# Routing of a mixture-of-experts stage: bf16 marks scanned before the matmul, slot tile by rounding, one comparison per row, and work of the next stages moved

## The chip, the cores and the metric

One core of one Trainium2 chip. The metric is device time in microseconds (us) of one execution of the whole program, as the median of several; lower is better.

## The reference

Two layers over x of 4 batches x 512 tokens x 256, each with cross attention and then a feed-forward part. The part that matters here is the feed-forward part of the first layer: eight experts, each token goes to the one with the largest router output.

```python
x = x + jnp.tanh(g_xattn[0]) * _L0_xattn_ref(_layernorm(x), ctx_768, ...)
x = x + jnp.tanh(g_ffn[0])   * _L0_ffn_ref(_layernorm(x), ...)       # the experts
x = x + jnp.tanh(g_xattn[1]) * _L1_xattn_ref(_layernorm(x), ctx_768, ctx_768, ...)
x = x + jnp.tanh(g_ffn[1])   * _L1_ffn_ref(_layernorm(x), ...)

def _L0_ffn_ref(hidden_states, router_w, router_b, w1, w2):
    logits = x @ router_w + router_b
    route = jax.nn.softmax(logits, axis=1)
    max_prob = jnp.max(route, axis=1, keepdims=True)
    max_ind = jnp.argmax(route, axis=1)
    for e in range(num_experts):                     # 8 experts, 256 -> 2 x 1024 -> 256
        a, g = jnp.split(x @ w1[e], 2, axis=1)
        y = jax.nn.silu(a) * g @ w2[e]
        out = jnp.where((max_ind == e)[:, None], y, out)
    return out * max_prob
```

## The kernel before

The 2048 tokens are 16 tiles of 128 (`NT` = 16; a batch is `TB` = 4 tiles). Each engine has its own written program in one block (`@block.tensor`, `@block.vector`, `@block.scalar`, `@block.gpsimd`, `@block.sync`); an engine runs its instructions in the order in which they are written, and waits on semaphores where the code says `wait_ge`. There is no scheduler: where a line stands in an engine's program is where it runs.

The stages are: attention of layer 0 (`attention(0, b, ...)` for b = 0 to 3), in which each batch ends with normalised rows `xn2` (they are also stored to `token_rows` in HBM) and router products of the batch before; routing; the experts; gathering of their outputs; attention of layer 1; the last feed-forward part.

Routing sorts the tokens by expert. `logits` [128, tile, expert] give `onehot`, the mark of each token's expert. A matmul with `before` (1 above the diagonal) counts the marks of earlier tokens in the same tile, one with `ones` the marks of each tile; DVE copies the latter to `count` and scans it over the tiles to `upto`. From `upto` follow the number of 128-row slot tiles of each expert (`tiles_of`, `tile_end`, `slot_base`), and from all of it the position `pos_f` of each token in the sorted list. The list has at most 24 slot tiles (25 are read, `READ_TILES`). To invert it, the kernel makes `in_slot` (bf16, 1 where a token has a given slot within its tile) and `ids` (tile number and row number of the token in the column of its slot tile) and lets PE multiply them: 16 matmuls into `x_bank[0]`, which give `token_f` and `token_of`, the token of each slot. POOL makes the half of `ids` with the row numbers (L573), in the same interval as DVE makes the other.

POOL then gathers the rows of the first two slot tiles by indirect DMA (`gather_rows`), PE turns them (`rows_in`, L960), ACT rounds them to `xs_hi` (L1279), DVE makes the rest `xs_lo` (L1756), and PE starts the first expert product (L976). Every fp32 product with expert weights is made as three products of a high and a low part; ACT makes the high parts of the weights (`upper_first` L1254, `upper_second` L1260), DVE the low parts (`lower_first` L1746, `lower_second` L1751). For the first expert all of that lies between the routing and the first expert tile; ACT's high parts stand behind its copy of the router rows and the exponent `l_exp` (L1248), DVE's low parts behind `token_of` (L1740).

Other work of PE in the stretch: the values of layer 1 (`values_of`, L681 and L682, four batches; DVE spreads them by `spread_values`, L1464), the keys of layer 1 (`keys(1, t_bank)`, L674 and L676; ACT copies them, then makes `k_bd`), and `keep_running(n, o)`: n matmuls of 512 columns whose result nobody reads. Last, SP loads the weights of experts 0 and 1 in this stretch and, when `r_exps` is 2, starts the loop over the later experts.

## Time and profile before

| | us |
|---|---|
| median of 3 runs | 603.48 |
| lowest, highest | 597.16, 603.55 |
| the profiled execution | 595.08 |
| its span, first to last instruction | 592.7 |
| mean granted PE clock (share of full speed) | 0.927 |
| PE busy | 499.5 (84%) |
| DVE busy | 419.2 (71%) |
| ACT busy | 294.2 (50%) |
| POOL busy | 247.1 (42%) |

PE is TensorE, DVE is VectorE, ACT is ScalarE, POOL is GpSimd and SP is SyncE. The profile is of one execution. A timeline row gives the start from the beginning of the span, the time from the first start to the last end of a merged group, the engine, the line of the kernel, the operation and its tiles, and in brackets how long the engine was idle before it and which instruction released it. `x8` means eight instructions in one row. Tiles that share memory are named by one name: `bank`, `s_tile` and `xn` appear for several views, `h_t` for `in_slot` and `ids`, `ew` for the expert weights and for `xn2`.

### The profile page before, as it was taken

Reading aid. Unit: us, or ns where it says so; the run is one execution under the profiler, and the core shown is the slowest. Engines: PE = TensorE matmul, PEld = TensorE weight load, DVE = VectorE, ACT = ScalarE, POOL = GpSimd, SP = SyncE. Lnnn points to the kernel's source line nnn. Section 1 sums busy time; section 2 is a strip of 40 time slices with the busy share of each in tenths; the row PEclk is TensorE's granted clock in tenths of the full one; section 3 lists DMA queues with packets and bytes.
Section 4 is the critical chain, followed back from the end, with each engine's and each line's share of the span. In section 5 each row is a group of like instructions: output and inputs, shape, how many; then the busy total and the mean of one; then the engine's idle time right before and its main releaser. Section 6 shows DMA issues by size and latency. Waiting matters only on the chain.

```text
span 592.7 us, 10230 instructions
## 1 busy us (share of the span) xinstructions
PE 499.5 (84%) x3061; PEld 364.4 (61%) x3069; DVE 419.2 (71%) x809; ACT 294.2 (50%) x521; POOL 247.1 (42%) x314
## 2 busy tenths in 40 slices
PE   7888899896998699899999999944897777649994
PEld 3456658566784278788888888812553544425562
DVE  6598898787546987494756823227979899588992
ACT  1446555362654466483755623203454444427884
POOL 5454263344300311020212110066367878538996
PEclk9989899699698899899999999979599989588999
DMA  7940100100167156555554310022000000000112
GB/s 212 296 147 1 37 0 2 36 0 1 35 215 236 31 161 221 180 178 168 174 178 154 94 35 18 18 81 71 0 1 1 1 1 1 0 0 2 36 35 71
DMA packets 35162, 46.40 MB, mean 78 GB/s; under 512 B 2764, under 2 KB 25304, under 8 KB 35128
## 3 DMA queue, kind: packets, MB, share of 16 engines
q1 hardware_dynamic: 30856, 39.02, 20.4%
q0 software_dynamic: 1680, 4.59, 2.7%
q10 hardware_dynamic: 2592, 2.36, 1.2%
q8 instruction: 18, 0.29, 0.2%
q14 instruction: 16, 0.13, 0.1%
HBM read 38.36 MB, written 7.60 MB: 78 GB/s over the span
## 4 chain that ended last, share of the span: by engine, by line
PE 45%; DVE 28%; POOL 10%; issue 7%; ACT 3%; DMA 2%; SPq 2%; DVEq 1%; POOLq 0%; ACTq 0%
PE s_tile L976 16%; PE bank L997 8%; DVE s_max L1476 4%; DVE p_sum L1490 4%; PE bank L827 3%; DVE probs L1481 3%; PE bank L986 3%; DVE stats L1414 2%; DVE xn L1436 2%; DVE ew L1436 2%; PE bank L711 2%; PE s_tile L1070 2%; POOL probs_t L614 2%; DMA w<-in_L_xattn_W 2%; DVE ew_lo L1746 2%
## 5 line engine op out<-in xcount | busy, mean ns | idle before, releaser
L506 POOL TENSOR_TENSOR probs<-probs,p_rcp 128x1024 f32<-128x1024 f32 x32 | 60.9, 1907 | 94.3 <-DVE p_rcp L1493 94.3
L740 PE MATMUL bank<-ident,probs 128*128 128x128 f32 x256 | 40.4, 309 | 27.0 <-POOL probs L506 25.3
L976 PE MATMUL s_tile<-ew_hi,xs_hi 128*128 128x512 f32 x144 | 59.9, 416 | 3.7 <-DVE ew_lo L1746 2.5
L1167 ACT COPY probs_t<-bank 128x512 f32<-128x512 f32 x64 | 35.0, 588 | 47.1 <-PE bank L740 46.7
L976 PE MATMUL s_tile<-ew_hi,xs_lo 128*128 128x512 f32 x144 | 57.5, 399 | 0.0
L976 PE MATMUL s_tile<-ew_lo,xs_hi 128*128 128x512 f32 x144 | 57.4, 398 | 0.0
L740 PEld LDWEIGHTS bank<-ident,probs 128*128 128x128 f32 x256 | 32.9, 159 | 39.5 <-POOL probs L506 30.1
L564 POOL TENSOR_TENSOR token_now<-token_of,carried 128x1 uint32<-128x1 uint32 x17 | 3.8, 226 | 124.1 <-PE bank L960 124.1
L1764 DVE TENSOR_TENSOR probs_t<-s_tile,probs_t 128x512 f32<-128x512 f32 x36 | 24.8, 689 | 43.1 <-PE s_tile L976 41.7
L1137 ACT ACTIVATE probs<-probs 128x1024 f32<-128x1024 f32 x32 | 33.9, 1058 | 33.8 <-DVE probs L1481 33.7
L1476 DVE TENSOR_REDUCE s_max<-s_tile 128x16 f32<-128x1024 f32 x32 | 38.4, 1199 | 16.6 <-PE s_tile L724 16.5
L1746 DVE TENSOR_TENSOR ew_lo<-ew,ew_hi 128x512 fp32r<-128x512 f32 x64 | 40.4, 686 | 10.3 <-ACT ew_hi L1254 9.4
L1490 DVE TENSOR_REDUCE p_sum<-probs 128x16 f32<-128x1024 f32 x32 | 38.7, 1209 | 6.4 <-ACT probs L1137 6.3
L724 PE MATMUL s_tile<-k_bd,q_t 64*128 64x256 f32 x256 | 40.6, 433 | 3.0 <-ACT q_t L1132 3.0
L997 PE MATMUL bank<-ew_hi,act_hi 128*128 x144 | 42.2, 293 | 0.0
L1481 DVE TENSOR_TENSOR probs<-s_tile,s_max 128x1024 f32<-128x1024 f32 x32 | 39.2, 1225 | 2.0 <-DVE s_max L1476 0.3
L997 PE MATMUL bank<-ew_lo,act_hi 128*128 x144 | 40.5, 282 | 0.0
L997 PE MATMUL bank<-ew_hi,act_lo 128*128 x144 | 40.3, 280 | 0.0
L1254 ACT CAST ew_hi<-ew 128x512 fp32r<-128x512 f32 x64 | 35.5, 619 | 7.5 <-issue 7.5
L1768 DVE TENSOR_TENSOR act_lo<-bank,act_hi 128x512 fp32r<-128x512 f32 x36 | 24.8, 689 | 18.6 <-ACT act_hi L1295 18.6
L1295 ACT CAST act_hi<-bank 128x512 fp32r<-128x512 f32 x36 | 21.2, 588 | 30.4 <-PE bank L986 30.4
L1285 ACT ACTIVATE probs_t<-s_tile 128x512 f32<-128x512 f32 x36 | 21.5, 599 | 28.3 <-PE s_tile L976 24.6
(228 smaller groups left out, 1318.8 us busy)
## 6 DMA issues: line engine op xcount, KB each, us to landing
ew<-in_L_ffn_w SPq DMA_DIRECT2D x32, 512.0 KB, 5.0
...
```

Of the source, the lines that this page charges most:

```text
L506: nc.gpsimd.tensor_tensor(p, p, p_rcp[:, i, :].unsqueeze(2).to_broadcast([P, H, M]), ALU.mult).then_inc(s["p_norm"], 1)
L724: last = nc.tensor.matmul(s_bank[i % 2][g][:, GH * M * m:GH * M * m + GH * M], q_t[rows, m, P * i:P * i + P], flat(k_bd[rows, m, bass.ds(n ...
L740: last = nc.tensor.transpose(t_bank[c][:, P * j:P * j + P], probs[:, i % 2, at:at + P], ident[:])
L976: last = nc.tensor.matmul(o[:], x, w, start=(k == 0 and n == 0), stop=(k == DK - 1 and n == 2))
L997: last = nc.tensor.matmul(y_bank[:, D * par:D * par + D], u, w, start=(c == 0 and n == 0), stop=(c == EK - 1 and n == 2))
L1137: nc.scalar.activation(probs[:, i % 2, :], probs[:, i % 2, :], ACT.Exp).then_inc(att[l]["a_exp"], 1)
L1167: last = nc.scalar.copy(flat(probs_t[:, i % 2, 4 * c:4 * c + 4, :]), t_bank[c][:])
L1254: last = nc.scalar.copy(hi, w)
L1476: nc.vector.tensor_reduce(s_max[:, i, :], s_tile[i % 2][:].rearrange("p (h s) -> p h s", h=H), AX, ALU.max).then_inc(s["v_max"], 1)
L1481: nc.vector.tensor_tensor(probs[:, i % 2, :].rearrange("p (h s) -> p h s", h=H), s_tile[i % 2][:].rearrange("p (h s) -> p h s", h=H), s_ma ...
L1490: nc.vector.tensor_reduce(p_sum[:, i, :], probs[:, i % 2, :].rearrange("p (h s) -> p h s", h=H), AX, ALU.add).then_inc(s["v_sum"], 1)
L1746: last = nc.vector.tensor_tensor(lo, w, hi.bitcast(F32), ALU.subtract)
```

## The change

Routing:

- the marks (`onehot`), `before`, a new `ones_b` and `upto` are bf16. DVE scans the marks themselves over the tiles, row by row, into `upto`, and PE sums that over the 128 rows: two matmuls with `ones_b`, the first added into the same bank as the one with `before`, so that the bank holds the position within the expert at once; the second gives each expert's total. The copy to `count` and two steps on `r_tmp` are gone;
- the slot tile of a position is found by scaling, shifting and rounding (adding and subtracting `ROUND`), in two steps over 16 elements, in place of a comparison with 26 edges and a sum. `in_tile` is then one comparison;
- `in_slot` is made by 16 operations of 128 elements with a per-row scalar, from a bf16 list of slot numbers, in place of four over 512 elements;
- the table of experts by slot tile (`past`, `expert_f`, `last_of`, `expert_of`), `pos` and `weight` come behind the token matmuls or behind `token_of`.

Moved:

- ACT's high parts of the first expert's first weights come ahead of the last router rows; keys come ahead of its second weights;
- DVE's low parts of the first expert, parts 0 to 2, come ahead of the last logits; part 3 stays behind the routing;
- PE makes the values of batches 0 and 1, then the keys, ahead of the last router rows (in other banks), the values of batches 2 and 3 behind the token matmuls; fillers are 6 and 5, 10, 6 where they were 10, 8, 14. A wait for the residual (`v_y`) at the end of the last batch is gone and a full one stands before the keys.

```diff
@@ PE
-                pe.wait_ge(s["v_y"], TB * b + 2)
+                if not (l == 0 and last_batch):
+                    pe.wait_ge(s["v_y"], TB * b + 2)
...
-            for b in range(B):
-                values_of(1, b, s_bank[1][b // 2])
+            for b in range(2):
+                values_of(1, b, s_bank[1][0])
+            pe.wait_ge(att[0]["v_y"], NT)
+            keys(1, (x_bank[0], s_bank[1][1]))
             pe.wait_ge(a_bit, 6)
-            keep_running(10, s_bank[0][0])
-            pe.wait_ge(att[0]["v_y"], NT)
+            keep_running(6, s_bank[0][0])
             router_turn(B - 1)
             router_products(B - 1)
+            keep_running(5, s_bank[0][0])
             pe.wait_ge(r_hot, 1)
-            nc.tensor.matmul(s_bank[0][0][:, 0:NT * E], before[:], flat(onehot[:]), start=True, stop=True)
-            nc.tensor.matmul(s_bank[0][1][:, 0:NT * E], ones[:], flat(onehot[:]), start=True,
-                             stop=True).then_inc(r_mm, 1)
-            keys(1, t_bank)
-            keep_running(8, x_bank[1])
+            nc.tensor.matmul(s_bank[0][0][:, 0:NT * E], before[:], flat(onehot[:]), start=True, stop=False)
+            pe.wait_ge(r_hot, 2)
+            nc.tensor.matmul(s_bank[0][0][:, E:NT * E], ones_b[:], upto[:, :, 0:NT - 1].rearrange("p e t -> p t e"),
+                             start=False, stop=True)
+            nc.tensor.matmul(s_bank[0][1][:, 0:E], ones_b[:], upto[:, :, NT - 1:NT].rearrange("p e o -> p (e o)"),
+                             start=True, stop=True).then_inc(r_mm, 1)
+            pe.wait_ge(r_lg, B)
+            keep_running(10, x_bank[1])
+            pe.wait_ge(a_k, 2 * DK)
...
             last.then_inc(r_mm, 1)
-            pe.wait_ge(a_k, 2 * DK)
-            keep_running(14, x_bank[1])
+            for b in range(2, B):
+                values_of(1, b, s_bank[1][1])
+            keep_running(6, x_bank[1])
             pe.wait_ge(v_vbd, 8)
@@ ACT
-            router_rows(B - 1)
-            act.wait_ge(r_v, 2)
-            nc.scalar.activation(l_exp[:], r_tmp[:], ACT.Exp).then_inc(r_exp, 1)
...
+            act.wait_ge(att[0]["t_y"], NT)
             for p in range(4):
                 upper_first(0, 0, p)
+            router_rows(B - 1)
+            act.wait_ge(r_v, 3)
+            nc.scalar.activation(l_exp[:], r_tmp[:], ACT.Exp).then_inc(r_exp, 1)
+            act.wait_ge(p_kbd, DK * B)
+            keys(1, (x_bank[0], s_bank[1][1]))
             for q in range(2):
                 upper_second(0, 0, q)
@@ DVE
+            spread_values(1, 0, s_bank[1][0])
+            for p in range(3):
+                lower_first(0, 0, p)
             router_logits(B - 1)
...
+            for e in range(E):
+                last = nc.vector.tensor_tensor_scan(upto[:, e, :], onehot[:, :, e], zeros[:, 0:NT], 0.0, ALU.add,
+                                                     ALU.add)
+            last.then_inc(r_hot, 1)
...
+            nc.vector.tensor_scalar(slot_tile[:], pos_f[:], 1.0 / P, -(P / 2 - 0.5) / P, ALU.mult, ALU.add).then_inc(r_v, 1)
+            nc.vector.tensor_scalar(slot_tile[:], slot_tile[:], ROUND, -ROUND, ALU.add, ALU.add).then_inc(r_v, 1)
+            nc.vector.tensor_tensor(in_tile, slot_tile_no[:].unsqueeze(1).to_broadcast([P, NT, READ_TILES]),
+                                    slot_tile[:].unsqueeze(2).to_broadcast([P, NT, READ_TILES]),
+                                    ALU.is_equal).then_inc(r_v, 1)
...
-            for b in range(B):
-                nc.vector.tensor_tensor(in_slot[:, TB * b:TB * b + TB, :],
-                                        pos_lo[:, TB * b:TB * b + TB].unsqueeze(2).to_broadcast([P, TB, P]),
-                                        slot_no[:].unsqueeze(1).to_broadcast([P, TB, P]), ALU.is_equal).then_inc(r_slot, 1)
+            for t in range(NT):
+                last = nc.vector.tensor_scalar(in_slot[:, t, :], slot_no_b[:], pos_lo[:, t:t + 1], None, ALU.is_equal)
+                if t % TB == TB - 1:
+                    last.then_inc(r_slot, 1)
...
+            nc.vector.tensor_copy(pos[:], pos_f[:])
+            spread_values(1, 1, s_bank[1][1])
+            nc.vector.tensor_scalar(weight[:], l_sum[:], tg[:, 2:3], None, ALU.mult)
+            nc.vector.tensor_scalar(wd_g[:], w_mean[:, 2:3], tg[:, 3:4], None, ALU.mult).then_inc(v_wm, 1)
@@ POOL
-            pool.wait_ge(r_v, 25)
+            pool.wait_ge(r_v, 18)
```

The orders on PE and DVE follow. First PE from the last batch's second product on, before (`h_t` is `in_slot` and `ids`, `wva` and `wvb` belong to the values, `wka` and `wkb` to the keys; L648 are the fillers):

```order
L681 MATMUL s_tile<-wva,ctx_ta 128x256
L682 MATMUL s_tile<-wvb,ctx_tb 128x256
L648 MATMUL s_tile<-ident_b 128x512 x10
L881 MATMUL bank<-ident,ew 128x128 x8
L888 MATMUL bank<-rw,xn_t 128x8 x8
L933 MATMUL s_tile<-onehot,before 128x128
L934 MATMUL s_tile<-onehot,ones 128x128
L674 MATMUL bank<-ctx_ta,wka 128x256
L676 MATMUL bank<-ctx_tb,wkb 128x256
L674 MATMUL bank<-ctx_ta,wka 128x256
L676 MATMUL bank<-ctx_tb,wkb 128x256
L648 MATMUL bank<-ident_b 128x512 x9
```

The same place in the changed kernel:

```order
L681 MATMUL s_tile<-wva,ctx_ta 128x256
L682 MATMUL s_tile<-wvb,ctx_tb 128x256
L674 MATMUL bank<-ctx_ta,wka 128x256
L676 MATMUL bank<-ctx_tb,wkb 128x256
L674 MATMUL s_tile<-ctx_ta,wka 128x256
L676 MATMUL s_tile<-ctx_tb,wkb 128x256
L648 MATMUL s_tile<-ident_b 128x512 x6
L882 MATMUL bank<-ident,ew 128x128 x8
L889 MATMUL bank<-rw,xn_t 128x8 x8
L648 MATMUL s_tile<-ident_b 128x512 x5
L936 MATMUL s_tile<-onehot,before 128x128
L938 MATMUL s_tile<-upto,ones_b 128x120
```

Keys moved up from behind the counts to ahead of the router rows, two of the four value groups moved down behind the token matmuls, and the second matmul on the marks became two on `upto`.

DVE around the logits, before:

```order
L1464 TENSOR_TENSOR v_blk<-s_tile,bv 64x16x16 x4
L1534 TENSOR_TENSOR logits<-bank,rb 128x32
L1648 TENSOR_SCALAR wd_g<-w_mean,tg 128x1
L1651 TENSOR_REDUCE l_max<-logits 128x16
L1653 TENSOR_TENSOR r_tmp<-logits,l_max 128x128
L1656 TENSOR_TENSOR onehot<-logits,l_max 128x128
L1659 SCALAR_TENSOR_TENSOR count<-onehot,expert_no 128x128
L1663 TENSOR_REDUCE first<-count 128x16
```

and in the changed kernel:

```order
L1470 TENSOR_TENSOR v_blk<-s_tile,bv 64x16x16 x2
L1654 TENSOR_TENSOR ew_lo<-ew,ew_hi_58 128x512
L1654 TENSOR_TENSOR ew_lo<-ew,ew_hi_55 128x512
L1654 TENSOR_TENSOR ew_lo<-ew,ew_hi_58 128x512
L1654 TENSOR_TENSOR ew_lo<-ew,ew_hi_55 128x512
L1654 TENSOR_TENSOR ew_lo<-ew,ew_hi_58 128x512
L1654 TENSOR_TENSOR ew_lo<-ew,ew_hi_55 128x512
L1540 TENSOR_TENSOR logits<-bank,rb 128x32
L1668 TENSOR_REDUCE l_max<-logits 128x16
L1670 TENSOR_TENSOR onehot<-logits,l_max 128x128
```

Six low parts (L1654 is `lower_first`) now stand where the second half of the spread stood, and `wd_g` is gone from here.

DVE from the final marks to the position sum, before:

```order
L1665 TENSOR_TENSOR onehot<-expert_no,first 128x128
L1669 TENSOR_REDUCE l_sum<-l_exp 128x16
L1671 RECIPROCAL l_sum<-l_sum 128x16
L1673 TENSOR_SCALAR weight<-l_sum,tg 128x16
L1676 COPY count<-s_tile 128x128
L1679 SCALAR_TENSOR_TENSOR upto<-count,x_res 128x16 x8
L1684 TENSOR_TENSOR more<-upto,tile_edge 128x128
L1687 TENSOR_REDUCE tiles_of<-more 128x8
L1689 TENSOR_SCALAR tiles_of<-tiles_of 128x8
L1691 SCALAR_TENSOR_TENSOR tile_end<-tiles_of,x_res 128x8
L1694 TENSOR_TENSOR past<-tile_end,slot_tile_no 128x192
L1697 TENSOR_TENSOR slot_base<-tile_end,tiles_of 128x8
```

and in the changed kernel:

```order
L1681 TENSOR_TENSOR onehot<-expert_no,first 128x128
L1685 SCALAR_TENSOR_TENSOR upto<-onehot,x_res 128x16 x8
L1690 TENSOR_REDUCE l_sum<-l_exp 128x16
L1692 RECIPROCAL l_sum<-l_sum 128x16
L1695 TENSOR_TENSOR more<-s_tile,tile_edge 128x128
L1698 TENSOR_REDUCE tiles_of<-more 128x8
L1700 TENSOR_SCALAR tiles_of<-tiles_of 128x8
L1702 SCALAR_TENSOR_TENSOR tile_end<-tiles_of,x_res 128x8
L1704 TENSOR_TENSOR slot_base<-tile_end,tiles_of 128x8
L1707 SCALAR_TENSOR_TENSOR r_tmp<-slot_base,s_tile 128x128
```

The scans come directly behind the final marks, the copy to `count` is gone, and between `tile_end` and the step on `r_tmp` only `slot_base` is left (the order names a scan SCALAR_TENSOR_TENSOR).

DVE from the token list on, in the changed kernel:

```order
L1739 CAST token_of<-xn 128x25
L1740 TENSOR_REDUCE expert_f<-past 128x24
L1741 TENSOR_SCALAR last_of<-tile_end 128x8
L1743 CAST expert_of<-expert_f 128x24
L1744 CAST pos<-pos_f 128x16
L1470 TENSOR_TENSOR v_blk<-s_tile,bv 64x16x16 x2
L1746 TENSOR_SCALAR weight<-l_sum,tg 128x16
L1747 TENSOR_SCALAR wd_g<-w_mean,tg 128x1
L277 TENSOR_LOAD last_of
L277 ISA x2
L1654 TENSOR_TENSOR ew_lo<-ew,ew_hi_58 128x512
L1654 TENSOR_TENSOR ew_lo<-ew,ew_hi_55 128x512
```

Before, the row behind `token_of` was L277, then eight low parts and `xs_lo`; now the expert table, the second spread (L1470) and two scalings stand ahead of L277, and two low parts behind it.

## Rows read from the trace of the kernel before

**Rows 1.** Page, part 4: shares of the chain that ended last, by engine

```profile
PE 45%; DVE 28%; POOL 10%; issue 7%; ACT 3%; DMA 2%; SPq 2%; DVEq 1%; POOLq 0%; ACTq 0%
```

**Rows 2.** Timeline of PE: start us, us, engine, line, operation, tiles, shapes, count [idle before]

```profile
175.33 0.70 PE L681 MATMUL s_tile<-wva,ctx_ta 128*128 128x256 f32 x2 [0.44 <-DVE x_res L1621]
...
180.36 2.33 PE L648 MATMUL s_tile<-ident_b 128*128 128x512 bf16 x10
182.53 1.04 PE L881 MATMUL bank<-ident,ew 128*128 128x128 f32 x8
184.29 1.95 PE L888 MATMUL bank<-rw,xn_t 128*128 128x8 f32 x16 [0.73 <-ACT xn_t L1142]
...
189.83 1.22 PE L676 MATMUL bank<-ctx_tb,wkb 64*128 64x256 f32 x2
```

**Rows 3.** Timeline of DVE, the routing stretch, same columns

```profile
180.71 1.77 DVE L1464 TENSOR_TENSOR v_blk<-s_tile,bv 64x256 f32<-64x256 f32 x4
186.28 0.19 DVE L1534 TENSOR_TENSOR logits<-bank,rb 128x32 f32<-128x32 f32 x1 [3.79 <-PE bank L888]
...
188.00 0.29 DVE L1665 TENSOR_TENSOR onehot<-expert_no,first 128x128 f32<-128x128 f32 x1
...
189.42 0.80 DVE L1679 TENSOR_TENSOR_SCAN upto<-count,x_res 128x16 f32<-128x16 f32 x8
190.26 0.29 DVE L1684 TENSOR_TENSOR more<-upto,tile_edge 128x128 f32<-128x128 f32 x1
...
191.11 0.17 DVE L1691 TENSOR_TENSOR_SCAN tile_end<-tiles_of,x_res 128x8 f32<-128x8 f32 x1
...
192.97 0.29 DVE L1709 SCALAR_TENSOR_TENSOR r_tmp<-slot_base,r_tmp 128x128 f32<-128x128 f32 x1
...
193.62 0.29 DVE L1714 TENSOR_REDUCE pos_f<-r_tmp 128x16 f32<-128x128 f32 x1
...
195.06 0.57 DVE L1722 TENSOR_TENSOR xn<-xn 128x400 f32<-128x400 f32 x1
...
196.16 3.15 DVE L1732 TENSOR_TENSOR h_t<-pos_lo,slot_no 128x512 bf16<-128x512 f32 x4
...
199.89 0.21 DVE L1737 TENSOR_REDUCE xn<-bank 128x25 f32<-128x50 f32 x1 [0.50 <-PE bank L946]
200.14 0.18 DVE L1740 CAST token_of<-xn 128x25 uint32<-128x25 f32 x1
201.07 4.91 DVE L1746 TENSOR_TENSOR ew_lo<-ew,ew_hi 128x512 fp32r<-128x512 f32 x8 [0.75 <-issue]
205.89 0.42 DVE L1756 TENSOR_TENSOR xs_lo<-bank,xs_hi 128x256 fp32r<-128x256 f32 x1
```

**Rows 4.** Timelines of ACT and POOL, same stretch and columns

```profile
187.37 4.24 ACT L1254 CAST ew_hi<-ew 128x512 fp32r<-128x512 f32 x8
...
205.15 0.37 ACT L1279 CAST xs_hi<-bank 128x256 fp32r<-128x256 f32 x1 [7.59 <-PE bank L960]
...
195.71 1.24 POOL L573 TENSOR_TENSOR h_t<-xn,row_no 128x400 bf16<-128x400 f32 x1 [16.43 <-DVE pos_lo L1725]
```

**Rows 5.** Instructions of two lines: ns min/median/max, first and last start us, forms

```profile
L1732 DVE TENSOR_TENSOR h_t<-pos_lo,slot_no x4: 677/680/1343, 196.2 to 198.6; 128x512 bf16<-128x512 f32 x4
...
L1508 DVE TENSOR_SCALAR bo<-bo,tg x2: 342/428/514, 32.1 to 32.5; 128x256 f32<-128x256 f32 x2
```

**Rows 6.** Timeline of DVE in the first layer, columns as before

```profile
32.08 0.78 DVE L1508 TENSOR_SCALAR bo<-bo,tg 128x256 f32<-128x256 f32 x2
...
149.50 1.22 DVE L1530 TENSOR_SCALAR ew<-ew 128x2048 f32<-128x2048 f32 x1
```

**Rows 7.** Stretches: length, busy us of each engine, granted PE clock, DMA share, GB/s

```profile
189.00:193.30 4.30, 4.30 (x10) 1.70 (x9) 3.90 (x23) 4.30 (x8) 0.00 (x0) 0.50 0.99 344
193.30:196.50 3.20, 3.10 (x9) 0.97 (x8) 3.10 (x8) 3.17 (x9) 0.79 (x1) 0.61 0.04 12
...
206.40:209.00 2.60, 2.60 (x6) 2.11 (x7) 2.60 (x3) 2.48 (x4) 0.74 (x1) 0.50 0.24 57
```

173 lines of the change are left out of this document (74 added, 99 removed).

## The prediction

> **What bounds the kernel now.** The page's chain of waits comes first: no engine owns the end, 45% of it is PE, 28% DVE, 10% POOL [rows 1]. So a stage is worth what its own chain holds, and the timelines of the stage have to be read. The change touches one stage, the routing between the last batch of the first attention layer and the first expert tile. I read PE's timeline there [rows 2], then DVE's [rows 3], then what ACT and POOL give to it [rows 4].
>
> The stage is one serial line. PE does values for the second layer from 175.33, then ten filler matmuls from 180.36 (2.33 us, 0.226 each start to start), and only at 182.53 turns the normalised rows, though DVE had them ready at about 180.7, where it goes on to L1464. ACT copies, PE makes the logits from 184.29 to 186.24 [rows 2], and DVE adds the bias at 186.28. From there DVE is the line: 13.6 us until it reads the token list at 199.89 [rows 3]. Then POOL's gather starts, and 5.75 us after token_of (200.14) DVE starts xs_lo at 205.89 [rows 3], on which the first expert matmul waits. ACT had xs_hi at 205.15 + 0.37 = 205.52 [rows 4], so xs_lo was held 0.37 us by the eight L1746 subtractions before it. The reader should see that ACT and POOL idle and that PE's work here is small: every step taken off DVE's line moves the end of the kernel by its own length, as long as nothing else becomes last.
>
> **The change, part by part** (times are start to start; a dependent DVE step costs its duration plus some 0.03 us: 0.32 for 128 elements, 0.20 for 8 or 16, from the distances in [rows 3]).
>
> (a) *To the logits.* PE now has four value groups instead of eight (0.63 each: eight lie between 175.33 and 180.36), then four groups of keys, then six fillers. Its wait for two residual steps is gone and with it the 0.44 of idle before 175.33 [rows 2], so it starts at 174.9: 174.9 + 8 x 0.63 + 6 x 0.226 = 181.3. It turns rows 1.2 us earlier than 182.53, and the product would be ready at 185.0. But DVE first does two spreads (1.77 / 4 each) and six subtractions L1746 (4.91 for eight, 0.61 each) [rows 3]: 180.71 + 0.88 + 3.66 = 185.25. DVE is last now. Logits at 185.3 instead of 186.28: -1.0. ACT's casts for them take 4.24 us [rows 4] and start when PE's second product ends, about 174.9, so they are done by 179.2 and the copy of the router rows at 182 waits for nothing.
>
> (b) *Logits to `more`.* Before 3.98 us (186.28 to 190.26) [rows 3]. The count copy goes (0.32), the weight scaling moves back, onehot now precedes r_tmp (0.11 of a wait saved), and the scans run on the marks right behind onehot, so the PE round trip (188.31 to 189.10 before) lies under l_sum and its reciprocal. New line: 1.60 to the final onehot, 0.33, 0.81 of scans, 0.31 and 0.20 of the sum and reciprocal, = 3.25: -0.7. The bf16 matmuls are new in this form; if they took as long as the fp32 ones (0.8 us), `more` came 0.3 later.
>
> (c) *`more` to the position sum.* Before 190.26 to 192.97 = 2.71. The expert table, its reduction and cast, and two r_tmp steps leave the line; between tile_end (191.11) and 192.97 only slot_base and one step of 0.20 remain: 0.41 in place of 1.86. -1.45.
>
> (d) *Position sum to in_slot.* From pos_f 193.62 to 196.16 = 2.54 before [rows 3]. Comparison and reduction over 416 elements become two steps over 16 (0.52 with pos_f's own 0.32), 0.20, then in_tile 0.49, pos_lo 0.11 and ids 0.50 as now: 1.83. -0.7.
>
> (e) *in_slot to the token list.* Before 196.16 to 199.89 = 3.73: a first piece of 1343 ns while POOL's L573 ran, and three of 0.60 [rows 3, 4, 5], then 0.58 of PE. Now sixteen one-row scalar comparisons with a pointer operand in bf16. This form is not in the trace. The nearest row is L1508: 128x256 fp32 with a pointer, two in 0.78 of which the second is 514 ns, so 0.266 start to start [rows 5, 6]. An fp32 scalar operation moves two elements a cycle (2048 in 1.22 us [rows 6]), so 0.133 of it is length and 0.133 fixed. For 128 elements: 0.20, so 16 make 3.2 us; POOL's hold of 0.66 stays and PE's 0.58 too: 4.45, +0.7. The bounds: 0.10 each, the pace of the 16-element scans [rows 3], makes 1.6, with PE's group of some 0.4 as the limit behind it: -0.8. At 0.266 each, as though nothing were saved by the shorter row: 4.26, +1.8. I take the middle one.
>
> The Trainium skill's "VectorE: DVE Perf Modes", "The perf-mode tier table", gives such an operation four elements a cycle when everything is bf16 in SBUF. By it a row would cost 0.17, (e) would be +0.2, and the total 0.5 us better than mine; no run here shows the form.
>
> (f) *Token list to xs_lo.* Before 5.75 us. The gather and the two engines behind it need 5.38 (200.14 to 205.52). On DVE, the small steps (0.8) are followed by a wait for the values of batches 2 and 3, which PE now computes behind the token matmuls: 4 x 0.63 = 2.5 us from the end of those, then two spreads 0.88, two scalings 0.4, the issue gap 0.75 and two subtractions 1.2: 5.5 from token_of. PE's own wait for the spreads ends 1 us before the gathered rows come. So -0.25, with nothing to spare.
>
> Sum: -1.0 - 0.7 - 1.45 - 0.7 + 0.7 - 0.25 = **-3.4 us**. What is costed at nothing: POOL's constants (its wait for DVE's first statistics covers them), the late table for SP (it waits for the first experts' products), keys' copies on ACT. Everything after xs_lo only moves. The sum stands against the profiled execution's 595.08 us (span 592.7), which is 8.4 under the median of the three runs, 603.48; they lie 6.39 apart. Applied to the median: 600.1.
>
> **The rivals.**
>
> *PE's clock falls and the moved work pays it.* The granted clock is 0.50 in 189.00 to 193.30, after the narrow router products and an idle stretch, and keys took 1.22 a group there [rows 2, 7]. In (f) the values then take 4 x 1.15 = 4.6 us, 2.1 more, with DVE and PE waiting behind them. Against it: 0.61 in the next stretch shows it rising [rows 7], and ten fillers stand ahead of the token matmuls. Result -1.3: 602.2. Chance 0.25.
>
> The Trainium skill's "TensorE: Matmul & The Clock Gate", "Part 1: The HAM clock gate", says a busy-ness monitor sets the rate; by that rule too the sparse stretch here would bring the low rate, and the times would be those of this rival. The trace agrees that the level falls after sparse work.
>
> *The marks are not cheaper and ids comes late.* If POOL's L573 (1.24 us [rows 4]) does not get in between sixteen short operations, the token matmuls start after all of them: 3.2 + 0.66 + four groups at 0.45, so token list at 5.7, +2.0 instead of +0.7. Against: POOL got in at 195.71 and DVE waited. Result -2.1: 601.4. Chance 0.12.
>
> *The cheap marks.* Rows at 0.10 to 0.17 make -3.9 to -4.9: 598.6 to 599.6. Chance 0.15.
>
> *Slower than before.* The clock falls ahead of the values and is still low through the first expert tiles. It was 0.50 in 206.40 to 209.00 already [rows 7]; a second low stretch as long as the one from 189.00 (over 4.3 us) in dense expert matmuls costs half its length, 2.2, above the 2.1: +0.9, 604.4. It decides only if both fall together. Chance 0.06.
>
> **How the numbers follow.** My forecast, -3.4, has 0.42. The low end of the range is not the sum but the runs: a median of three can land at either end of 597.16 to 603.55. 597.16 less 4.9 is 592.3; the high end is the slower rival, 604.4. The mechanism's own range is 598.6 to 602.2. A measurement here tells about 1% (6 us) from no change. No case of mine is a gain of 6 us; faster by over 1% comes from the scatter of the runs alone, if the median falls at their low end (half of the four executions shown lie there), 0.36. Slower by over 1% needs the last rival and the scatter: 0.03. The rest, 0.61, is within 1%.
>
> **What would show it.** In the trace after: turned rows near 181.3, logits near 185.3 with DVE and not PE last; `more` 3.25 us later; 0.41 between tile_end and the position sum; sixteen comparisons 0.20 apart; token list near 196.7; L1464's second pair waiting for PE, and xs_lo near 202.5. The prediction is wrong if the comparisons are over 0.3 apart, if the values run at the low clock, or if xs_lo comes over 6 us behind token_of.

## The result, and the profile after

The changed kernel takes 592.3 us (median of 20 runs, 587.6 to 600.21), the kernel before 598.62 us (20 runs beside it, 592.3 to 603.55). The ratio is 0.992, 95% interval 0.9894 to 0.9945: 4.8 us less (3.3 to 6.3), within 1% of no change. Timed a second time it was 0.992 again (0.988 to 0.9959). The ratios are those of the fast runs, which leaves out the runs over 1.5% above the fastest of the same kernel, 4 of the 20 here and 3 of the 20 before.

The profiled execution took 592.3 us: span 590.5, mean granted PE clock 0.926, against 592.7 and 0.927. The shares of the chain of waits, against [rows 1]:

```profile
PE 43%; DVE 33%; POOL 9%; issue 8%; ACT 4%; DVEq 1%; DMA 1%; POOLq 0%; ACTq 0%
```

PE's share is lower by 2% of the span and DVE's higher by 5%, some 30 us, which is more than the whole stage lasts. So these shares are no measure of this change, and the stage has to be read by itself.

DVE's timeline of the routing stretch in the changed kernel, same columns as [rows 3] (`ew<-x_res` are the normalised rows, L1729 makes `in_slot`, L1736 reads the token list):

```profile
182.64 1.38 DVE L1442 TENSOR_SCALAR ew<-x_res,mv,rstd 128x256 f32<-128x256 f32 x4 [1.51 <-POOL rstd L405]
183.93 0.86 DVE L1470 TENSOR_TENSOR v_blk<-s_tile,bv 64x256 f32<-64x256 f32 x2
184.83 3.70 DVE L1654 TENSOR_TENSOR ew_lo<-ew,ew_hi 128x512 fp32r<-128x512 f32 x6
188.56 0.19 DVE L1540 TENSOR_TENSOR logits<-bank,rb 128x32 f32<-128x32 f32 x1
...
191.78 0.29 DVE L1695 TENSOR_TENSOR more<-s_tile,tile_edge 128x128 f32<-128x128 f32 x1
...
192.63 0.17 DVE L1702 TENSOR_TENSOR_SCAN tile_end<-tiles_of,x_res 128x8 f32<-128x8 f32 x1
192.84 0.17 DVE L1704 TENSOR_TENSOR slot_base<-tile_end,tiles_of 128x8 f32<-128x8 f32 x1
193.04 0.29 DVE L1707 SCALAR_TENSOR_TENSOR r_tmp<-slot_base,s_tile 128x128 f32<-128x128 f32 x1
...
195.53 3.28 DVE L1729 TENSOR_SCALAR h_t<-slot_no_b,pos_lo 128x128 bf16<-128x128 bf16 x16
...
199.40 0.21 DVE L1736 TENSOR_REDUCE xn<-bank 128x25 f32<-128x50 f32 x1 [0.32 <-PE bank L952]
199.64 0.18 DVE L1739 CAST token_of<-xn 128x25 uint32<-128x25 f32 x1
...
201.80 0.88 DVE L1470 TENSOR_TENSOR v_blk<-s_tile,bv 64x256 f32<-64x256 f32 x2 [1.45 <-PE s_tile L682]
...
204.69 0.42 DVE L1751 TENSOR_TENSOR xs_lo<-bank,xs_hi 128x256 fp32r<-128x256 f32 x1 [0.43 <-ACT xs_hi L1285]
```

To compare executions, each step is measured from the start of the normalised rows, which is 179.41 before and 182.64 here. The table puts the prediction's terms beside both traces, start to start in us; "STT" is the step on `r_tmp` that adds `slot_base` (L1709 before, L1707 here).

| term | before | after | predicted | measured |
|---|---|---|---|---|
| (a) normalised rows to logits | 6.87 | 5.92 | -1.0 | -0.95 |
| (b) logits to `more` | 3.98 | 3.22 | -0.7 | -0.76 |
| (c) `more` to STT | 2.71 | 1.26 | -1.45 | -1.45 |
| (d) STT to `in_slot` | 3.19 | 2.49 | -0.7 | -0.70 |
| (e) `in_slot` to token list | 3.73 | 3.87 | +0.7 | +0.14 |
| token list to `token_of` | 0.25 | 0.24 | 0 | -0.01 |
| (f) `token_of` to `xs_lo` | 5.75 | 5.05 | -0.25 | -0.70 |
| sum | 26.48 | 22.05 | -3.4 | **-4.43** |

The spans of this pair differ by 2.2 only, since PE's clock fell early in the changed kernel's execution, in code that the change leaves alone. PE's timeline of the first layer, before:

```profile
12.30 0.70 PE L682 MATMUL s_tile<-wvb,ctx_tb 64*128 64x256 f32 x2
...
16.10 3.67 PE L711 MATMUL bank<-xn_t,wq 128*128 128x512 f32 x8 [0.82 <-ACT xn_t L1127]
```

and after:

```profile
12.16 1.22 PE L682 MATMUL s_tile<-wvb,ctx_tb 64*128 64x256 f32 x2
...
18.34 5.68 PE L711 MATMUL bank<-xn_t,wq 128*128 128x512 f32 x8 [0.77 <-ACT xn_t L1134]
```

PE's granted clock was 1.00 from 12 to 20 us before, and 0.54 (12 to 14 us) and 0.50 (14 to 20 us) here. The same matmuls lie 4.3 us later by the end of L711's group, and the normalised rows 3.23 later. What follows `xs_lo` took 386.81 before and 385.81 after. So 3.23 - 4.43 - 1.0 = -2.2. It is the stage, not the span of one pair, that shows the change, and the 20 runs beside 20 agree with it: -4.8 by time, -4.43 by the stage.

PE's clock in the stage, windows of the changed kernel (length, busy us of each engine, granted PE clock, DMA share, GB/s), for [rows 7]:

```profile
188.00:190.00 2.00, 0.99 (x5) 0.26 (x3) 1.87 (x7) 0.37 (x2) 0.00 (x0) 0.91 0.99 301
190.00:192.00 2.00, 0.95 (x5) 0.42 (x6) 1.88 (x13) 2.00 (x4) 0.00 (x0) 0.50 1.01 376
...
194.00:196.00 2.00, 2.00 (x5) 0.45 (x3) 1.92 (x6) 1.75 (x5) 0.92 (x1) 0.50 1.09 348
196.00:198.00 2.00, 0.93 (x11) 0.54 (x10) 2.00 (x12) 0.00 (x0) 0.32 (x1) 0.88 0.20 66
198.00:200.00 2.00, 1.68 (x16) 0.94 (x14) 1.65 (x11) 0.00 (x0) 0.00 (x0) 1.00 0.00 0
200.00:203.00 3.00, 3.00 (x12) 1.20 (x11) 1.48 (x9) 0.00 (x0) 1.95 (x2) 1.00 0.11 23
```

The clock falls to 1.2 GHz shortly before 190, in the 1.5 us that PE idles in front of the counting matmuls, so the ten fillers behind these run at half clock (4.43 us). It is back at 2.4 GHz before the moved values start at 199.20.

### The profile page after: what moved, and what is told of

It is laid out like the page before. It is cut to its first block, busy times and chain, and to the rows that moved or that the text cites. A ratio compares the mean times of both kernels' runs of the same rounds, so it can differ in the third digit from the quotient of the medians.

```text
span 590.5 us, 10228 instructions
## 1 busy us (share of the span) xinstructions
PE 495.0 (84%) x3055; PEld 359.7 (61%) x3063; DVE 417.2 (71%) x818; ACT 293.6 (50%) x521; POOL 246.6 (42%) x315
## 3 DMA queue, kind: packets, MB, share of 16 engines
q0 software_dynamic: 1680, 4.59, 2.8%
## 4 chain that ended last, share of the span: by engine, by line
PE 43%; DVE 33%; POOL 9%; issue 8%; ACT 4%; DVEq 1%; DMA 1%; POOLq 0%; ACTq 0%
PE s_tile L983 16%; PE bank L1004 8%; DVE s_max L1482 5%; DVE p_sum L1496 5%; DVE probs L1487 4%; PE bank L827 3%; PE bank L711 3%; DVE stats L1420 3%; PE bank L993 3%; DVE ew L1442 2%; DVE xn L1442 2%; POOL probs_t L614 2%; DVE x_res L1627 2%; DVE ew_lo L1654 1%; PE s_tile L1077 1%
## 5 line engine op out<-in xcount | busy, mean ns | idle before, releaser
L983 PE MATMUL s_tile<-ew_hi,xs_hi 128*128 128x512 f32 x144 | 58.5, 406 | 3.4 <-DVE ew_lo L1654 2.5
L740 PE MATMUL bank<-ident,probs 128*128 128x128 f32 x256 | 38.8, 300 | 25.7 <-POOL probs L506 22.7
L983 PE MATMUL s_tile<-ew_lo,xs_hi 128*128 128x512 f32 x144 | 56.2, 391 | 0.0
L740 PEld LDWEIGHTS bank<-ident,probs 128*128 128x128 f32 x256 | 31.7, 154 | 37.5 <-POOL probs L506 29.3
L1654 DVE TENSOR_TENSOR ew_lo<-ew,ew_hi 128x512 fp32r<-128x512 f32 x64 | 40.5, 687 | 9.6 <-ACT ew_hi L1256 9.4
L724 PE MATMUL s_tile<-k_bd,q_t 64*128 64x256 f32 x256 | 39.3, 422 | 3.0 <-ACT q_t L1139 3.0
L711 PE MATMUL bank<-xn_t,wq 128*128 128x512 f32 x64 | 34.6, 684 | 6.4 <-ACT xn_t L1134 4.6
```

The lines of the kernel that those rows point to most:

```text
L711: last = nc.tensor.matmul(x_bank[m][:], wq[l][:, k, m * P:m * P + P], xn_t[:, k, :], start=(k == 0), stop=(k == DK - 1))
L724: last = nc.tensor.matmul(s_bank[i % 2][g][:, GH * M * m:GH * M * m + GH * M], q_t[rows, m, P * i:P * i + P], flat(k_bd[rows, m, bass.ds(n ...
L740: last = nc.tensor.transpose(t_bank[c][:, P * j:P * j + P], probs[:, i % 2, at:at + P], ident[:])
L983: last = nc.tensor.matmul(o[:], x, w, start=(k == 0 and n == 0), stop=(k == DK - 1 and n == 2))
L1654: last = nc.vector.tensor_tensor(lo, w, hi.bitcast(F32), ALU.subtract)
```

## The experiments

All stages in one table, in us. A column that isn't shown, (b) to (d), is 3.21 to 3.22, 1.26 to 1.27 and 2.48 to 2.49 in every kernel with the new chain. "Rows" is the time of the sixteen comparisons, or of the four. Where a kernel ran once, its time is given but decides nothing: the runs of the kernel before alone lie between 592.3 and 603.55. The stage decides.

| kernel | (a) | rows | (e) | (f) | sum |
|---|---|---|---|---|---|
| before | 6.87 | 3.15 | 3.73 | 5.75 | 26.48 |
| changed | 5.92 | 3.28 | 3.87 | 5.05 | 22.05 |
| changed, again | 5.93 | 3.29 | 3.87 | 5.04 | 22.05 |
| new chain, places of before | 6.85 | 3.28 | 4.75 | 6.79 | 25.61 |
| the same, again | 6.92 | 3.29 | 4.99 | 6.80 | 25.92 |
| four wide comparisons | 5.92 | 3.15 | 4.05 | 5.27 | 22.46 |
| fp32 slot list | 5.92 | 3.81 | 4.59 | 7.15 | 24.89 |
| ids on ACT | 5.93 | 2.69 | 3.27 | 5.09 | 21.51 |
| low parts behind | 5.29 | 3.28 | 4.15 | 8.83 | 25.48 |
| both spreads behind | 5.29 | 3.29 | 4.16 | 5.19 | 21.85 |
| no fillers | 5.94 | 3.28 | 4.15 | 5.50 | 22.80 |
| values as fillers | 5.93 | 3.29 | 4.22 | 5.07 | 22.45 |
| ids, spreads, values together | 5.30 | 2.69 | 4.94 | 5.04 | 22.50 |
| ids and spreads | 5.32 | 2.69 | 3.27 | 5.02 | 20.82 |

### Is it the new chain or the moves?

The changed kernel with PE's, ACT's and DVE's work at the places of before (four values and ten fillers ahead of the last rows, keys and eight fillers behind the counts, ACT's high parts and DVE's eight low parts behind); the arithmetic of the routing stays the changed one, and so does the place of the expert table, `pos` and the two scalings behind the token matmuls:

```diff
-            for b in range(2):
-                values_of(1, b, s_bank[1][0])
-            pe.wait_ge(att[0]["v_y"], NT)
-            keys(1, (x_bank[0], s_bank[1][1]))
+            for b in range(B):
+                values_of(1, b, s_bank[1][b // 2])
...
-            keep_running(10, x_bank[1])
-            pe.wait_ge(a_k, 2 * DK)
+            keys(1, t_bank)
+            keep_running(8, x_bank[1])
...
-            lower_first(0, 0, 3)
+            for p in range(4):
+                lower_first(0, 0, p)
```

> The new routing chain with the placement of before: values of all batches and fillers ahead, keys behind the counts, both spreads ahead of the logits, all eight low parts behind the routing, ACT's high parts behind its exponent. Theory: from the start of the normalised rows (xn, 4 instructions) to the logits 6.9 us (before 6.87, changed 5.92); logits to token_f 10.8 as in the changed kernel (10.84; before 13.61); token_of to xs_lo 6.3, since small steps (0.65), the issue gap (0.75) and eight subtractions (4.91) stand ahead of it: 24.2 in all against 26.48 before and 22.05 changed. So the chain alone is worth 2.2 and the moves 2.2. Rival: the moves are what is worth, by the clock or by a free DVE during POOL's gather; then the chain alone is within 1 us of before.

It took 599.88 us in one run, the kernel before beside it 600.44. The same kernel was then timed in more runs, and the changed kernel, with no edit, beside it:

> The new chain with the placement of before, timed. Its trace gave xn to xs_lo 25.61, of which 0.88 was a fallen clock in the token matmuls. Theory by the steps: 24.7 with PE's clock full, so 1.8 us faster than before, a ratio of 0.997, and 2.6 slower than the changed kernel. Rival: the chain is the whole gain, ratio 0.992.

> The changed kernel itself beside e10 and e12 on the same chip. Theory: ratio 0.992 against before as measured, e10 1 to 2 us below it. Its trace is a second sample of the clock: xn to logits, to more, to the position sum and to in_slot 5.92, 3.22, 1.26 and 2.49 again within 0.02, since they hold no wide matmul; in_slot to token_f 3.9 to 4.6 and token_of to xs_lo 5.05 to 7.15 by the clock. Rival: these vary too, and the sum of the steps was one execution's luck.

The chain alone: 597.64 us (12 runs) against 599.1 (21 runs), ratio 0.9986 (0.9949 to 1.0024). The changed kernel in the same set: 595.31 (10 runs), 0.992 (0.988 to 0.9959), and its stage the same to 0.01 in every term. By time the chain alone isn't told from no change, and its interval touches the changed kernel's; what follows is read from the stage. The chain alone was expected to give more than it did. PE's timeline of it shows why:

```profile
191.48 1.20 PE L674 MATMUL bank<-ctx_ta,wka 128*128 128x256 f32 x2
...
194.91 1.22 PE L676 MATMUL bank<-ctx_tb,wkb 64*128 64x256 f32 x2
196.06 3.26 PE L648 MATMUL bank<-ident_b 128*128 128x512 bf16 x9
199.16 0.26 PE L948 MATMUL bank<-h_t 128*128 128x50 bf16 x4
```

and DVE's:

```profile
195.42 3.29 DVE L1722 TENSOR_SCALAR h_t<-slot_no_b,pos_lo 128x128 bf16<-128x128 bf16 x16
...
200.41 0.21 DVE L1729 TENSOR_REDUCE xn<-bank 128x25 f32<-128x50 f32 x1 [1.44 <-PE bank L948]
...
202.63 4.91 DVE L1648 TENSOR_TENSOR ew_lo<-ew,ew_hi 128x512 fp32r<-128x512 f32 x8 [1.02 <-issue]
207.46 0.42 DVE L1743 TENSOR_TENSOR xs_lo<-bank,xs_hi 128x256 fp32r<-128x256 f32 x1
```

Keys at half clock and the fillers behind them keep PE until 199.16, 17.6 us after the normalised rows (181.54), while `in_slot` starts at 13.9. Before, it started only at 16.75, and PE stood idle when its first piece was done. DVE now waits 1.44 for the token matmuls (+1.3 in (e), +1.0 in the first trace). It is this queue and not, as the second expectation has it, a fallen clock in the token matmuls themselves: they ran 0.32 apart. Besides, the expert table and the small steps ahead of the eight low parts move these, and with them `xs_lo`, by 1.0 in (f). Of the 2.9 us that (b), (c) and (d) win, 0.6 to 0.9 are left. The moves take both off: by the stage they are worth 3.6 to 3.9 us beside the new chain. The moves with the old chain weren't tried.

### Low parts behind the routing again

```diff
-            for p in range(3):
-                lower_first(0, 0, p)
             router_logits(B - 1)
...
-            lower_first(0, 0, 3)
+            for p in range(4):
+                lower_first(0, 0, p)
```

> The changed kernel with all four low parts of the first expert behind the routing; spreads, values and keys stay as changed. Theory: the logits come 0.65 us earlier (PE then is last: its product ended 0.67 before DVE was free), and xs_lo comes later by six subtractions (3.7) less the 0.43 that DVE had spare: 3.3; net 2.6 us worse than changed, xn to xs_lo 24.7. Second point: POOL's two gather instructions, 1.62 and 1.23 us before and 1.23 and 0.95 in the changed kernel. If eight subtractions on DVE beside them are the cause, they are long again only if the subtractions start before them; here DVE waits for the second values first, so the first one stays 1.23 and the second may be longer.

594.06 us in one run. (a) falls by 0.63 and no more: PE's product ended 0.04 before the logits, where it ended 0.67 before them in the changed kernel. So six low parts (3.70 us) ahead of the logits cost 0.63, and behind `token_of` they cost 3.78. Net 3.4 us, 0.8 more than expected. Most of the excess is the clock: the token matmuls ran at the low level (their fillers 0.6 each) for 0.28 in (e), and with the first group of values at 1.10 the second spread came 2.56 behind `token_of` instead of 2.16. The sum up to `xs_lo` doesn't hold all of it: DVE's next step on the first expert's products (`probs_t`) came 5.80 behind `xs_lo`, and 5.01 to 5.20 behind it in the other traces.

### The comparisons

Four comparisons of 512 in place of sixteen of 128:

```diff
-            for t in range(NT):
-                last = nc.vector.tensor_scalar(in_slot[:, t, :], slot_no_b[:], pos_lo[:, t:t + 1], None, ALU.is_equal)
-                if t % TB == TB - 1:
-                    last.then_inc(r_slot, 1)
+            for b in range(B):
+                nc.vector.tensor_tensor(in_slot[:, TB * b:TB * b + TB, :],
+                                        pos_lo[:, TB * b:TB * b + TB].unsqueeze(2).to_broadcast([P, TB, P]),
+                                        slot_no[:].unsqueeze(1).to_broadcast([P, TB, P]), ALU.is_equal).then_inc(r_slot, 1)
```

> The changed kernel with in_slot made as before, by four comparisons over 4x128 fp32. In the changed kernel the sixteen row comparisons took 3.28 us (one of 843 ns, the others 241 to 243), the four took 3.15 before. Theory: the sixteen gain nothing; from the start of in_slot to token_f it will be 3.7 to 3.8 us here against 3.87. Rival: the sixteen are dearer in the new surroundings or the four would be (POOL's product beside them); then the distance differs from 3.73 by over 0.3.

590.65 us in one run. And the slot list as fp32 in place of bf16:

```diff
-                last = nc.vector.tensor_scalar(in_slot[:, t, :], slot_no_b[:], pos_lo[:, t:t + 1], None, ALU.is_equal)
+                last = nc.vector.tensor_scalar(in_slot[:, t, :], slot_no[:], pos_lo[:, t:t + 1], None, ALU.is_equal)
```

> The changed kernel with the list of slot numbers in fp32 (the marks written stay bf16). Theory: with bf16 on both sides a row moves four elements a cycle (0.033 us for 128), with an fp32 list two (0.067); so a comparison lasts 0.24 + 0.03 = 0.27 us and the sixteen take some 0.5 us longer than 3.28. Rival: the fixed part of each instruction is all that counts, and nothing changes (under 0.1).

600.44 us in one run. The instructions of the line (ns min/median/max, first and last start), in the changed kernel:

```profile
L1729 DVE TENSOR_SCALAR h_t<-slot_no_b,pos_lo x16: 241/243/843, 195.5 to 198.6; 128x128 bf16<-128x128 bf16 x16
```

with the fp32 list:

```profile
L1729 DVE TENSOR_SCALAR h_t<-slot_no,pos_lo x16: 273/273/873, 197.3 to 200.9; 128x128 bf16<-128x128 f32 x16
```

and with the wide ones:

```profile
L1729 DVE TENSOR_TENSOR h_t<-pos_lo,slot_no x4: 677/680/1340, 190.5 to 193.0; 128x512 bf16<-128x512 f32 x4
```

In each the longest is the one that ran beside POOL's half of `ids`, by 0.60 to 0.66. In the changed kernel that product runs from 195.08 to 196.32, and the comparison that started at 195.53 ends 0.05 behind it. Without it, and without the last one's own time, the sixteen are (3.28 - 0.60 - 0.24) / 15 = 0.163 us apart in bf16, and (3.81 - 0.60 - 0.27) / 15 = 0.196 with the fp32 list, which costs 0.53 for the sixteen, as expected. The sixteen gain nothing on the four: 3.28 against 3.15. (e) is longer with the four (4.05) only because PE's token matmuls ran at the low clock there (fillers 0.60 each where they took 0.39).

The run with the fp32 list also shows the prediction's first rival. PE's timeline:

```profile
201.72 1.20 PE L681 MATMUL s_tile<-wva,ctx_ta 128*128 128x256 f32 x2
...
205.15 1.22 PE L682 MATMUL s_tile<-wvb,ctx_tb 64*128 64x256 f32 x2
206.31 2.36 PE L648 MATMUL bank<-ident_b 128*128 128x512 bf16 x6
208.50 0.38 PE L967 MATMUL bank<-ident,xs 128*128 128x128 f32 x2
```

and the same place in the changed kernel:

```profile
201.06 0.70 PE L682 MATMUL s_tile<-wvb,ctx_tb 64*128 64x256 f32 x2
201.69 1.47 PE L648 MATMUL bank<-ident_b 128*128 128x512 bf16 x6
203.81 0.44 PE L967 MATMUL bank<-ident,xs 128*128 128x128 f32 x2 [0.65 <-DMA xs<-token_rows,token_of]
```

DVE's, with the fp32 list:

```profile
202.18 0.18 DVE L1739 CAST token_of<-xn 128x25 uint32<-128x25 f32 x1
...
206.41 0.88 DVE L1470 TENSOR_TENSOR v_blk<-s_tile,bv 64x256 f32<-64x256 f32 x2 [3.54 <-PE s_tile L682]
...
209.33 0.42 DVE L1751 TENSOR_TENSOR xs_lo<-bank,xs_hi 128x256 fp32r<-128x256 f32 x1 [0.46 <-ACT xs_hi L1285]
```

and two of its windows:

```profile
198.00:200.00 2.00, 0.84 (x10) 0.52 (x10) 2.00 (x11) 0.00 (x0) 0.13 (x1) 1.00 0.10 33
...
202.00:204.00 2.00, 2.00 (x4) 0.70 (x3) 0.84 (x6) 0.00 (x0) 0.72 (x1) 0.50 0.00 0
```

With the values at half clock DVE waits 3.54 instead of 1.45, and (f) is 7.15 instead of 5.05: +2.1. DVE's wait isn't what ended last, though: `xs_lo` waits for ACT, and ACT for PE, which turned the gathered rows only behind its queue of values and six fillers. The values take 2.1 more (4.59 instead of 2.49 to the first filler), the fillers some 0.7 more, and 0.65 of idle time is used up. The clock had been back at 1.00 under the token matmuls and fell a second time. PE idled more there than in the changed kernel, because the fp32 rows come further apart: 1.12, 0.22, 0.29 and 0.29 in front of the four groups, against 0.99, some 0.1, 0.16 and 0.16. Whether that tipped it or chance did, one execution can't say.

### Fillers, and values in their place

Without the five and the ten fillers:

```diff
-            keep_running(5, s_bank[0][0])
...
-            keep_running(10, x_bank[1])
```

> The changed kernel without the five and the ten fillers around the counting matmuls. Nothing of the work is left out. Theory: PE is then nearly idle from the router products to the token matmuls (some 9 us), its granted clock is 0.50 at the token matmuls and in the values behind them: in_slot to token_f 4.2 or more (3.87), token_of to xs_lo 7.1 (5.05), xn to xs_lo 24.4 or more. This is the first rival of the prediction made to happen. Rival: the fillers are not what holds the clock; then xn to xs_lo stays within 0.5 of 22.05.

598.88 us in one run. The clock was low through the token matmuls and one and a half groups of values (1.20, 0.90, then 0.70 twice), and came back while the values ran. Against the changed kernel this is 0.28 in (e) and 0.45 in (f), a third of what was expected. Not even all of it is the price of the fillers: the kernels with the low parts behind and with both spreads behind keep them and lose the same 0.28 and 0.29 in (e), their token matmuls at the low level too. With the values of batches 2 and 3 in place of fillers:

```diff
-            keep_running(10, x_bank[1])
             pe.wait_ge(a_k, 2 * DK)
+            for b in range(2, B):
+                values_of(1, b, s_bank[1][1])
+            keep_running(4, x_bank[1])
...
-            for b in range(2, B):
-                values_of(1, b, s_bank[1][1])
-            keep_running(6, x_bank[1])
+            keep_running(14, x_bank[1])
```

> The changed kernel with the values of batches 2 and 3 in place of six of the ten fillers between the counts and the token matmuls (four fillers stay behind them), and fourteen fillers behind the token matmuls, as before the change. Theory: nothing of DVE's line waits for PE behind token_of any more: token_of to xs_lo is bound by the gather, 5.0 to 5.3, whether PE's clock is full or half in the values, and the second spread starts 0.65 us behind token_of. The gain over the changed kernel shows only where the clock falls (2.1 there); where it does not, 0. Rival: the values at half clock (4 x 1.15 = 4.6 us, as ten fillers took 4.43) hold the token matmuls; then in_slot to token_f grows over 3.87 by more than 0.5.

597.54 us in one run. DVE's wait of 1.45 for the second spread is gone, but that wait held nothing: `xs_lo` waits 2.01 for ACT now and (f) stays at 5.07. The values ran at half clock (1.20 and 1.22 a group, 193.67 to 198.3), and they and the fillers held the token matmuls: (e) +0.35.

### Two things taken off DVE's line, and a better kernel

The row-number half of `ids` on ACT (it takes 0.63 us there, beside the comparisons):

```diff
-            pool.wait_ge(r_v, 18)
-            nc.gpsimd.tensor_tensor(ids[:, :, 1, :], in_tile, row_no[:].unsqueeze(2).to_broadcast([P, NT, READ_TILES]),
-                                    ALU.mult).then_inc(p_tok, 1)
+            act.wait_ge(p_const, 15)
+            act.wait_ge(r_v, 18)
+            nc.scalar.activation(ids[:, :, 1, :], in_tile, ACT.Identity, scale=row_no[:, 0:1]).then_inc(p_tok, 1)
```

> The changed kernel with the row-number half of ids made by ACT (one activation over 400 elements with a per-row scale, behind k_bd) in place of POOL's product. Theory: the 843 ns comparison among the sixteen is DVE held for 0.60 us by POOL's product, which reads SBUF beside it; without POOL all sixteen last 241 to 243 ns, in_slot takes 2.7 in place of 3.28, and in_slot to token_f 3.3 in place of 3.87 where PE's clock is full. ACT is free at about the time (k_bd ends 0.2 us after in_slot starts), so its product ends 0.3 us before the first group of marks plus PE's wait. Rival: the long one is the first after a step that writes the same tile, whoever else runs; then it stays.

594.65 us in one run. The longest comparison is gone, (e) falls by 0.60. The spreads:

```diff
-            spread_values(1, 0, s_bank[1][0])
...
-            spread_values(1, 1, s_bank[1][1])
             nc.vector.tensor_scalar(weight[:], l_sum[:], tg[:, 2:3], None, ALU.mult)
             nc.vector.tensor_scalar(wd_g[:], w_mean[:, 2:3], tg[:, 3:4], None, ALU.mult).then_inc(v_wm, 1)
+            spread_values(1, 0, s_bank[1][0])
+            spread_values(1, 1, s_bank[1][1])
```

> The changed kernel with the spread of the first value pair moved from ahead of the low parts to behind the two scalings, next to the second spread. DVE was 0.67 us late for the logits and idle 1.45 us behind token_of, waiting for PE's values. Theory: xn to logits 5.29 (PE bound, as with the low parts behind), then the same chain, and token_of to xs_lo unchanged or up to 0.1 worse if PE's clock is full: it is bound there by the second values (2.2 us behind token_of), two spreads now one behind the other (one more 0.43 pair, 0.88), the issue gap and two subtractions: 2.15 + 1.75 + 0.75 + 1.2 = 5.85, less the 0.4 of scalings that move into the wait, 5.5 against 5.05. So about -0.65 + 0.45 = -0.2. Rival: the spread fits in DVE's wait whatever its order and all 0.65 are won.

592.59 us in one run. (a) falls by 0.63, and the first spread lies in DVE's wait for the second. 0.29 was lost in (e), where the token matmuls ran at the low clock, and 0.14 in (f). The net, -0.20, is the number expected, but by luck: DVE's line behind `token_of`, which was to cost 0.45, cost nothing (`xs_lo` waits 0.41 for ACT), and the clock took what it left. Both edits together with the values as fillers (the last three diffs in one kernel):

> The changed kernel with all three: ids on ACT, both spreads behind token_of, the second values in place of fillers. Theory: xn to logits 5.29, in_slot to token_f 3.3 to 3.6 by the clock, token_of to xs_lo 5.1 whatever the clock does in the values, xn to xs_lo 20.6 to 20.9 against 22.05 in the changed kernel and 26.48 before. So 1.2 to 1.4 us better than the changed kernel where its clock holds, up to 3.5 where it falls; against before about 6 us, a ratio of 0.990. Rival: DVE with two spreads behind token_of is last (0.65 + 0.4 + 1.75 + 0.75 + 1.2 = 4.75, so it should not be), then xs_lo comes over 5.4 behind token_of.

591.59 us (6 runs), ratio 0.9883 (0.9829 to 0.9936), but the stage is 22.50, no better than the changed kernel's. PE's timeline says where both gains went:

```profile
194.43 1.22 PE L679 MATMUL s_tile<-wvb,ctx_tb 64*128 64x256 f32 x2
195.58 2.32 PE L645 MATMUL bank<-ident_b 128*128 128x512 bf16 x5
197.69 0.38 PE L951 MATMUL bank<-h_t 128*128 128x50 bf16 x4
```

`in_slot` had started at 194.94, and its first four rows waited for PE until 197.69: (e) is 4.94. So the values went back behind the token matmuls, with the other two edits kept (the last two diffs):

> The changed kernel with two of the edits that had each shortened the stage alone: the row-number half of ids on ACT instead of POOL, and both spreads of the second layer's values behind token_of. PE's order stays that of the changed kernel, so, unlike in the kernel with the values of batches 2 and 3 ahead of the token matmuls, nothing at half clock stands in front of them. Theory (the steps add up, and what was lost there came from the values and fillers held ahead of the token matmuls): logits 5.3 after the normalised rows, then 3.22, 1.26 and 2.49 as in every trace; in_slot to token list 3.3, or up to 3.7 if the token matmuls fall at the low clock; token_of to xs_lo 5.1 to 5.3; normalised rows to xs_lo 20.7 to 21.1 against 22.05 of the changed kernel. The time is then about 1 us under the changed kernel's, ratio to the kernel before 0.990. Rival (the line is bound by PE from the position sum on, so that an earlier in_slot only waits): in_slot to token list over 4.2, the sum at 21.8 or more, and no gain over the changed kernel.

592.14 us (6 runs) against 598.28 (11 runs), ratio 0.9887 (0.9835 to 0.9938): 6.8 us less than before (3.7 to 9.9). DVE's timeline:

```profile
181.55 1.38 DVE L1443 TENSOR_SCALAR ew<-x_res,mv,rstd 128x256 f32<-128x256 f32 x4 [1.51 <-POOL rstd L405]
...
186.87 0.19 DVE L1541 TENSOR_TENSOR logits<-bank,rb 128x32 f32<-128x32 f32 x1 [0.32 <-PE bank L886]
...
193.83 2.69 DVE L1729 TENSOR_SCALAR h_t<-slot_no_b,pos_lo 128x128 bf16<-128x128 bf16 x16
...
197.10 0.21 DVE L1736 TENSOR_REDUCE xn<-bank 128x25 f32<-128x50 f32 x1 [0.32 <-PE bank L949]
...
202.37 0.42 DVE L1752 TENSOR_TENSOR xs_lo<-bank,xs_hi 128x256 fp32r<-128x256 f32 x1 [0.64 <-ACT xs_hi L1286]
```

The stage is 20.82 us. The single steps add up: 22.05 - 0.63 - 0.60 = 20.82. With PE's order as in the changed kernel only the ten fillers stand before the token matmuls. They run at half clock too (4.43 us), but end 0.39 before the first rows are there. It is one trace, in which the clock was back for the token matmuls. Against the kernel before it is faster by time, by 1.1%. Against the changed kernel the stage shows it, but the times don't yet: the intervals of the two ratios overlap.

## Why the prediction was right, and where a step failed

**The frame.** The stage is one line, mostly DVE's, and each step taken off it moves the end: right. The prediction's -3.4 stands beside -4.43 by the stage and -4.8 (3.3 to 6.3) by time. The time itself, 592.3, came 7.8 under the predicted 600.1, at the low end of the range. 4.9 of that is the level: the median that the sum was set against was 603.48 of three runs, and is 598.62 of 20. The other 2.9 is the difference of the two medians, 6.3, less the 3.4; the stage accounts for 1.0 of it, and for the other 1.9 no trace gives a cause. That the time lies in the range at all is luck: it falls on the low end, 592.3, which was set by the scatter of the runs, while the mechanism's own range was 598.6 to 602.2. The difference is what the prediction had right, and its two mis-sized terms, (e) and (f), erred the same way, by 0.56 and 0.45.

**(a) to (d).** Each within 0.06 us. DVE and not PE was last at the logits, as said: PE's product ended 0.67 before. Taking the low parts or the first spread from ahead of the logits won 0.63 each and no more, and PE was then last (0.04), which confirms it. Rows were turned 1.54 after the normalised rows instead of 3.12 (1.9 was forecast). The bf16 matmuls on the scans cost nothing visible: DVE reads them at `more` without a wait. 0.41 stood between `tile_end` and the step on `r_tmp`, as written.

**(e) was mis-sized.** The failed step is "0.133 of it is length ... For 128 elements: 0.20". The length was put at two elements a cycle. With the fp32 list that is what came (0.196), and in bf16 the rows were 0.163 apart. So (e) cost +0.14 and not +0.7, the case of the cheap marks, which had 0.15. The Trainium skill's "VectorE: DVE Perf Modes", "The perf-mode tier table", has four elements a cycle for this operation when all is bf16 in SBUF, and the estimate by it was 0.17 a row: the trace agrees, with 0.163. The rival in which POOL's product doesn't get in between short operations fell: it came beside the first of them, and held it 0.60.

**(f) was mis-sized.** The failed step is that DVE would be last, at 5.5 from `token_of`. It wasn't: DVE was free 4.61 behind `token_of` and then waited 0.43 for `xs_hi`. Its "issue gap 0.75" is not on the line: the register loads (L277) run beside the second spread, and so they do in the kernel with the values as fillers, where no wait stands ahead of the spread. The scalings took 0.26 and not 0.4, and PE started the values 0.44 before `token_of`, where 5.5 allowed some 0.25 (the terms as written add up to 5.7). What was last is POOL's first gather with the two engines behind it, and that was shorter than the 5.38 that the prediction took for a floor. POOL's timeline after:

```profile
200.75 1.23 POOL L558 DMA_INDIRECT xs<-token_rows,token_of  x1 [4.42 <-DVE token_of L1739]
202.28 0.95 POOL L558 DMA_INDIRECT xs<-token_rows,token_of  x1 [0.30 <-issue]
```

The first took 1.62 before, from 1.10 behind `token_of`, and 1.23 now, from 1.11: 0.39 less. ACT's `xs_hi` ends 5.01 behind `token_of` instead of 5.38, 0.37 less. The two agree, but the way from a gather's start to PE's turn of its rows scatters: where PE stood waiting for the rows it was 3.04 to 3.31 us with the same 1.23.

**The clock rival.** Its mechanism is real, and 2.1 us is what the values' low clock cost in the kernel with the fp32 list. That the number fits so well is in part luck: the six fillers behind the values were late by 0.7 as well, and idle time of 0.65 in front of the gathered rows covered that. In the changed kernel's two traces it did not happen. The fillers in front are not what decides it alone: without them only 0.73 was lost. With them all values ran at half clock once, and in the kernels with four wide comparisons, with the low parts behind and with both spreads behind the first group did (1.18, 1.10, 1.09). What tips it stays open.

**The slower rival.** It did not come, and its 2.2 for a low clock in the first expert products finds no support. Before, the clock was 0.50 in 206.40 to 209.00 [rows 7]; in the changed kernel it was 1.00 throughout. Yet DVE's next step on these products (`probs_t`) came 5.02 behind `xs_lo` before and 5.01 here.

**What no rival held.** The chain's gain hangs on the moves. Alone, the chain wins 2.9 us in (b) to (d) and gives back 2.1 to 2.3: 1.0 to 1.3 in (e), because PE's keys and fillers had been sized to the old chain, and 1.0 in (f), because the expert table and the small steps now stand ahead of eight low parts. The prediction's sum was for the whole and did not need that price, but it gave the reader no hint of it.
